# Gated attention block: three GpSimd adds per head and four ones-products per group, placed two score blocks later

## The reference, cut to what matters

```python
q = _qdq(x) @ _qdq(wq).T + bq
kv = cond @ wkv.T + bkv
k, v = jnp.split(kv, 2, axis=-1)
attn = jax.nn.softmax(jnp.einsum('bnhd,bmhd->bhnm', q, k) * scale, axis=-1)
o = jnp.einsum('bhnm,bmhd->bnhd', attn, v).reshape(B, N, C)
out = _qdq(o) @ _qdq(wp).T + bp
```

## Time and profile before

| | us |
|---|---|
| median of 3 runs | 1131.3 |
| lowest and highest of them | 1129.19, 1131.79 |
| the profiled execution, its own time | 1129.28 |
| span of its profile | 1127.5 |
| attention, first `s` to last `normalize` | 728.7 to 1010.7 |

### The profile page before, as it was taken

How to read it: one execution, slowest core, us unless ns; L and a number is a source line. 1 busy time by engine, 2 the same in 40 slices (tenths; PEclk the granted TensorE clock), 3 DMA queues, 4 the chain that set the end, 5 groups by cost and what they waited for, 6 DMA issues and landing times.

```text
span 1127.5 us, 15927 instructions
## 1 busy us (share of the span) xinstructions
PE 854.5 (76%) x4503; PEld 375.1 (33%) x4503; DVE 881.2 (78%) x1453; ACT 572.4 (51%) x1024; POOL 566.2 (50%) x559
## 2 busy tenths in 40 slices
PE   1376867672997888888888895589898898965654
PEld 1233534431443444444443343122232222222221
DVE  3859999994988988889888874577777777735985
ACT  1366969562443554445444455255555555644442
POOL 1166877861334444444444434264564655645652
PEclk9668889886998999999999998599999999986786
DMA  8422524330332322222222223212122121000011
GB/s 303 154 84 76 170 101 159 104 102 19 60 62 47 57 47 47 47 51 52 47 47 47 55 55 91 81 38 73 48 71 67 47 73 41 1 1 1 37 56 56
DMA packets 132708, 78.12 MB, mean 69 GB/s; under 512 B 90656, under 2 KB 115376, under 8 KB 132656
## 3 DMA queue, kind: packets, MB, share of 16 engines
q1 hardware_dynamic: 132656, 77.51, 25.6%
HBM read 37.50 MB, written 12.58 MB: 44 GB/s over the span
## 4 chain that ended last, share of the span: by engine, by line
DVE 41%; PE 26%; issue 16%; ACT 8%; SPq 4%; POOL 2%; DMA 1%; DVEq 1%; ACTq 0%; POOLq 0%
PE bank L1132 4%; DVE B L1532 4%; PE bank L1105 4%; DVE B L1422 4%; DVE B L1424 3%; DVE B L1427 3%; PE bank L1122 3%; PE bank L1037 3%; DVE B L1425 3%; SPq L403 3%; PE bank L1046 2%; DVE B L1339 2%; DVE B L1416 2%; DVE B L1433 2%; ACT B L791 2%
## 5 line engine op out<-in xcount | busy, mean ns | idle before, releaser
L1037 PE MATMUL bank<-A,B 128*128 128x512 f16 x1024 | 233.7, 382 | 15.4 <-DMA B<-B 15.4
L1532 DVE TENSOR_REDUCE B<-bank 128x1 f32<-128x512 f32 x256 | 163.4, 684 | 72.9 <-PE bank L1105 71.6
L878 ACT ACTIVATE A<-bank 128x512 f32<-128x512 f32 x256 | 138.9, 593 | 89.3 <-PE bank L1122 86.6
L531 POOL TENSOR_TENSOR B<-B 128x512 f16<-128x512 f32 x64 | 73.9, 1155 | 192.3 <-ACT B L768 89.4
L1037 PEld LDWEIGHTS bank<-A,B 128*128 128x128 f16 x1024 | 101.0, 99 | 140.0 <-issue 21.3
L613 POOL TENSOR_TENSOR B<-A 128x512 f32<-128x512 f32 x64 | 79.4, 1271 | 132.7 <-ACT A L878 132.7
L1046 PE MATMUL bank<-A,B 128*128 128x512 f16 x512 | 132.8, 407 | 1.3 <-DMA B<-B 1.3
L763 ACT ACTIVATE B<-B 128x512 f32<-128x512 f32 x64 | 40.4, 631 | 179.3 <-DVE B L1427 179.3
L1105 PE MATMUL bank<-A 96*128 96x512 f16 x256 | 101.0, 405 | 15.4 <-DVE B L1532 10.3
L1122 PE MATMUL bank<-A 98*128 98x512 f16 x256 | 96.6, 391 | 13.1 <-DMA A<-B 8.1
L1422 DVE SCALAR_TENSOR_TENSOR B<-bank,ffs,B 128x512 f32<-128x512 f32 x64 | 48.0, 751 | 50.4 <-PE bank L1037 24.1
(11 more groups left out here) (228 smaller groups left out, 1718.4 us busy)
## 6 DMA issues: line engine op xcount, KB each, us to landing
B<-in_L_ffn_w_dram SPq DMA_DIRECT2D x48, 256.0 KB, 3.3
A<-k_parts SPq DMA_DIRECT2D x48, 128.0 KB, 2.5
A<-B SPq DMA_DIRECT2D x192, 32.0 KB, 1.9
X<-in_x_dram SPq DMA_DIRECT2D x4, 1024.0 KB, 14.2
B<-in_ctx_dram SPq DMA_DIRECT2D x4, 1024.0 KB, 7.9
k_parts<-B SPq DMA_DIRECT2D x16, 256.0 KB, 2.2
v_rows<-B SPq DMA_DIRECT2D x16, 256.0 KB, 2.0
B<-v_rows SPq DMA_DIRECT2D x16, 256.0 KB, 3.2
```

The source lines that it names most:

```text
L531: nc.gpsimd.tensor_tensor(HLb[j][:, 1, :], Db[j % 2], HLb[j][:, 0, :], ALU.subtract).then_inc(lo_done, 1)
L878: nc.scalar.activation(PR[(HG * t + j) % 8], bank[2 + j % 2][:, :], ACT.Exp, scale=SCALE).then_inc(exp_done, 1)
L1037: last = mm(bank[2 * n + q][:, :], XQT[a][:, m, :], wt[:, m % DB, j * 512:j * 512 + 512], start=(m == 0), stop=(m == 2 * DB - 1))
L1532: reduce(NMX[:, t, j:j + 1], bank[n % 2][:, :], AX.X, ALU.max, negate=True).then_inc(row_max, 1)
```

## The change

1. GpSimd also adds key tile 3: steps t = 1, 2, 3, so 12 additions a group. All counts of `acc_done` follow (12 a group for 8).
2. `sum_weights` has four products, ACC by ones; the four with PR are gone.
3. ScalarE's exponentials of key tile 1 wait for the preceding group's additions of step 3 in place of `sum_ps`.
4. In `ORDER`, `a` leaves the first string and stands in the second, behind `o`, both ahead of that string's `v`; `d` leaves the end of the second string and stands in the third.
5. On VectorE `sums_out` comes after maximum n = 8 and `invert_sums` after n = 15, directly ahead of `max_parts`.

```diff
@@ add_weights (GpSimd)
-                    for t in (1, 2):
+                    for t in range(1, TB):
...
-                                pool.wait_ge(acc_done, n * 8 + j + 1)
+                                pool.wait_ge(acc_done, n * 12 + HG * (t - 2) + j + 1)
@@ attend (ScalarE)
-                            if t == 1:
-                                up_to(act, sum_ps, n)
+                            if t < 2:
+                                up_to(act, acc_done, n * 12 + j + (-7 if t == 0 else -3))
                             else:
-                                up_to(act, acc_done, n * 8 + (j - 3 if t == 0 else j + 1))
+                                up_to(act, acc_done, n * 12 + j + 1)
@@ sum_weights (TensorE)
-                pe.wait_ge(acc_done, n * 8 + 8)
+                pe.wait_ge(acc_done, n * 12 + 12)
...
-                    mm(bank[7][DH * j:DH * j + DH, :], ones[:, 0:DH], ACC[j], start=True, stop=False)
-                for j in range(HG):
-                    last_ = mm(bank[7][DH * j:DH * j + DH, :], ones[:, 0:DH], PR[HG * (TB - 1) % 8 + j], start=False, stop=True)
+                    last_ = mm(bank[7][DH * j:DH * j + DH, :], ones[:, 0:DH], ACC[j], start=True, stop=True)
@@ ORDER (TensorE)
-            ORDER = ("r r r v r a s r s r s s",
-                     "r s r s v r s r s r o d",
+            ORDER = ("r r r v r s r s r s s",
+                     "r s r s o a v r s r s r",
...
@@ attend (VectorE)
-                        if n == 5 and not opening:
+                        if n == 8 and not opening:
...
-                        if n == 12 and not opening:
+                        if n == 15 and not opening:
```

More of the change, by code:

```diff
@@ L1163, in sum_turn @@
                 last_.then_inc(s_ps, 1)
-            ORDER = ("r r r v r a s r s r s s",
-                     "r s r s v r s r s r o d",
-                     "r s r s v r s r s r",
+            ORDER = ("r r r v r s r s r s s",
+                     "r s r s o a v r s r s r",
+                     "r s r s v r s d r s r",
                      "s s v c s s")
```

## The result

| | before, us | after, us |
|---|---|---|
| median | 1130.5 | 1157.2 |
| lowest, highest (4 runs each) | 1129.2, 1131.8 | 1154.1, 1162.0 |
| the profiled execution | 1129.3 | 1157.7 |

The ratio is 1.0235, 95% interval 1.0215 to 1.0256: slower by 26.6 us, where 11.5 was forecast. The direction was right, the time lies 5 us beyond the range.

What follows compares the result with a forecast made beforehand. A ring of waits between VectorE and TensorE was taken as the bound. Period 18.1 us for 17.52 and the opening's 1.8 gain put the last S +6.8, the last group +4.7: +11.5 on 1131.3, so 1142.8; range 1134 to 1152.

Steps and rivals of the forecast that it cites:

- The ring of waits: Attention group: VectorE and TensorE's feeding order pace S (first `s`) to `c`, then TensorE or transfers; period 18.1 us for 17.52.
- The change-over rule: VectorE's cast and subtraction each wait for the running GpSimd addition (1.24 us) to end; `c` at S+14.5 for S+11.99.
- GpSimd not the bound, except at the end: Twelve additions take 14.9 us a group, leaving GpSimd 2 us to spare; only in the last group nothing covers them.
- The clock: Rival: TensorE's granted clock falls in the attention, 1.15 us a group, total 1159 us; chance 0.05.
- The last group: Nothing covers the additions: last S to the copy of the sums 21.0 us for 16.29, +4.7.
- The opening: Opening group has no `a`, so `c` stays and the next S comes 1.8 us earlier, gained once.
- missed change: Rival: VectorE's cast comes after GpSimd's change at S+13.18 and waits for the next; +1.24 us in 14 groups, 1160; chance 0.08.

Runs made afterwards that it cites:

- e2: Changed kernel with the copy of the sums after maximum n = 7 in place of n = 8; ratio 0.9997.
- e5: Kernel before with only VectorE's two placements: copy of the sums after n = 8, inversion after n = 15; ratio 1.0266.
- e3: Changed kernel with VectorE's cast and subtraction made by three reductions of one input each; ratio 0.9942.
- e9: Changed kernel with TensorE's order and VectorE's placements of the kernel before, leaving the arithmetic of the change alone; ratio 1.0434.
- e1: Changed kernel with five extra repeats of a product `s` in each group, in TensorE's wait ahead of `c`; ratio 1.0144.
- e10: Changed kernel with two extra repeats of a product `s` in each group, ahead of `c`; ratio 1.0183.
- e7: e5 with eight extra repeats of a product `s` ahead of `c`; ratio 1.0166.

## Why the prediction was right in its direction and wrong in its size

- **The ring of waits: right.** Period 18.1 forecast, 18.2 measured in undisturbed groups; `c` at S+14.5 and +14.59; c to S 3.6 and 3.5 to 3.6, the transfers and TensorE ready together: in groups 10 to 13 the weight load of the first `s` waits 0.23 to 0.26 us for them. That `o` and `a` ahead of `v` give VectorE idle time where it is missed (2.2 us forecast, 2.19 measured) was right too; this is read from the rows, no run moves them alone. In all the ring cost 10.3 us where 8.6 were forecast.
- **The change-over rule: right.** Confirmed by e2 (1.23 us from 0.60), e5 (1.2 from 0.3) and e3. From group 1 on the cast had 0.8 us of margin, where 0.45 was forecast, and missed no change.
- **GpSimd not the bound, except at the end: right.** It waited 57.2 us for `a` in groups 1 to 14. e9 shows what it costs where it is the bound.
- **The clock: this step failed.** The forecast priced it (1.15 us a group) and gave it 0.05, since "no gap longer than about 2 us arises". The earlier trace rows show TensorE's wait for `c`, 0.61 us; the walk moved `c` but never asked what that wait would become. It became 1.26. I asked only whether a long gap would appear, not whether one that every group has would double. The terms of that rival were off both ways: 1.15 us in each of 14 groups, where 2.0 us came in 4 of them. By e1 the clock is 10.3 us of the 26.6 by the medians, 7.8 by the profiled executions. That the time measured, 1157.2, lies so near to that rival's 1159 is in part luck: 16 for the clock were too much, and the ring, the last group and the opening cost more than forecast. The row that gave the price was misread, too: in the kernel before the clock was already at 0.50 ahead of the opening,

```profile
695.10:728.70 33.60, 15.38 (x49) 4.73 (x47) 16.64 (x28) 8.47 (x16) 12.86 (x10) 0.50 0.36 99
```

so the 0.54 of the earlier trace rows says nothing on what the wait of 8.06 us did.
- **The last group: mis-sized.** Forecast 21.0 from the last S to the copy of the sums, measured 23.56:

```profile
1013.20 1.03 PE L1122 MATMUL bank<-A 98*128 98x512 f16 x2
...
1017.82 1.94 PE L1142 MATMUL bank<-B,ones 128*32 128x512 f32 x8
...
1019.93 4.98 POOL L613 TENSOR_TENSOR B<-A 128x512 f32<-128x512 f32 x4 [6.02 <-PE bank L1142]
...
1034.76 1.93 PE L1142 MATMUL bank<-B,ones 128*32 128x512 f32 x8 [4.75 <-POOL B L613]
...
1036.76 0.69 DVE L1543 COPY B<-bank 128x512 f32<-128x512 f32 x1 [10.12 <-PE bank L1142]
```

  The twelve additions took what was forecast, 14.8 us. They started at S+6.73 for S+4.9, and from the last `a` to the copy it was 2.0 us for 1.2. The granted clock was 0.50 to 1021 and from 1031 us, and both `a` lie in those stretches; the forecast had `o` and `a` at full speed.
- **The opening: missed.** The gain of 1.8 became 0.4 lost in the profiled pair, by a clock that came up 5 us later. In e2, with the clock at 734, the gain is there: 16.61 us for 18.55. In the changed kernel the cast came just behind a change-over, 742.76 by the row of GpSimd, and waited for the next: the forecast's missed change, once.

```profile
740.29 6.17 POOL L613 TENSOR_TENSOR B<-B,A 128x512 f32<-128x512 f32 x5
...
742.82 1.23 DVE L1536 CAST B<-B 128x16 f16<-128x16 f32 x1
```

The sum without the clock's falls, 1.0144 or 1146.8 us, lies within the range; with them it is 5 us outside.

## What to carry to other kernels

Where one engine works in pieces of 1.2 us and another engine's small instructions wait for the end of a piece, as here, 0.3 us of delay can cost 1.2, and 0.6 us of work moved can gain 1.2; look for short instructions with long times that end together with the other engine's, and give them a form that doesn't wait. When a change lengthens a wait of TensorE, price the clock for every group, even for waits of about a microsecond: the cheapest test is to fill the wait with repeats of a product. And four products saved on a busy engine were worth nothing here, since they were saved in one place and what stayed was moved to another where the next engine runs dry.

## What was not expected of the hardware

- The granted clock fell behind waits of TensorE of 0.7 to 1.6 us: of groups 1 to 13 in 2 at 0.65 to 0.81 (e10), in 4 at 1.20 to 1.34 (the change) and in 9 at 1.56 to 1.65 (e5), and in none at 0.58 to 0.72 (before, e2). Why one group falls and the next, with the same waits, doesn't, stays open. The Trainium skill, TensorE: Matmul & The Clock Gate, section HAM oscillation, describes such falls behind waits for transfers in a loop; here the waits are shorter, and for VectorE.
- Useless products there made the kernel 10 us faster by the medians (e1), and e7 11 us faster than e5.
- In the opening group the same code brought the clock to 1.00 between 734 and 738 us in different executions, worth about 2.4 us (first to second S 16.61 in e2, 18.97 in the changed kernel).
